# Language-model tower on one core: identity products on TensorE moved in the first expert attention and added in the latent stage

## What is computed

```python
h = tok_embedding_with_layernorm(ids)            # 4096 tokens, 192 features
h = h + L0_attn(layernorm(h))                    # fake-quantised attention, 12 heads
h = h + L0_ffn(layernorm(h))                     # gate stage: 3 "experts" of causal attention, top-2 gate
h = h + L1_attn(layernorm(h))                    # latent stage
h = h + L1_ffn(layernorm(h))                     # routed stage: attention, then 8 experts, top 2

# L1_attn (latent stage)
latent = silu(rmsnorm(x) @ w_comp)               # 192 -> 128
q, k, v = split(latent @ w_qkv); gates from latent @ w_reso
out = decayed linear attention(q, k, v, gate)    # 12 heads of 16
x = x + rmsnorm(out) @ w_proj * silu(latent @ w_outgate)
x = x + (silu(xn @ w1) * (xn @ w2)) @ w3         # xn = rmsnorm(x), hidden 512

# L1_ffn (routed stage)
x = x + softmax(q k^T / 4) v @ out_proj          # 12 heads of 16, 128 tokens a sequence
xm = layernorm(x); top 2 of softmax(xm @ router) choose experts
x = x + sum of gelu(xm @ w1[e] + b1[e]) @ w2[e] + b2[e], weighted
```

## Time and profile before

| | |
|---|---|
| Three runs | 1986.03, 1988.45, 1989.02 us; median 1988.45 |
| Profiled execution: its own time | 1987.9 us |
| its span, first to last instruction | 1986.2 us, 36888 instructions |
| TensorE busy, share of the span | 1551.4 us, 78% |
| VectorE busy | 1311.0 us, 66% |
| ScalarE busy | 959.7 us, 48% |
| GpSimd busy | 400.6 us, 20% |
| Mean granted TensorE clock | 0.881 of full |

### The profile page before, as it was taken

One profiled execution on the slowest core, in us unless ns is written; L12 is line 12 of the kernel. 1 busy time (PEld: TensorE's weight loads), 2 busy tenths in 40 slices (PEclk: granted clock), 3 DMA queues, 4 the chain that ended last, 5 costly groups with the idle time before them and its releaser, 6 DMA issues.

```text
span 1986.2 us, 36888 instructions
## 1 busy us (share of the span) xinstructions
PE 1551.4 (78%) x12764; PEld 1187.1 (60%) x12764; DVE 1311.0 (66%) x4361; ACT 959.7 (48%) x2769; POOL 400.6 (20%) x494
## 2 busy tenths in 40 slices
PE   0076764888888667887888868999999949999996
PEld 0032221776666445565555546777777738888885
DVE  7898885787888768878888844666666632222221
ACT  1275999863444544454454423444434324444442
POOL 7401332000000100000000000222222223333332
PEclk9985555569999779989999988999999959999998
DMA  3000000119990000000000000000000027778875
GB/s 75 17 1 1 1 1 1 22 42 185 180 164 5 1 0 1 0 0 0 0 0 0 0 24 3 26 25 24 24 24 24 25 88 181 193 199 192 194 192 141
DMA packets 136264, 113.02 MB, mean 57 GB/s; under 512 B 29417, under 2 KB 128457, under 8 KB 136137
## 3 DMA queue, kind: packets, MB, share of 16 engines
q1 hardware_dynamic: 119320, 91.70, 20.2%
q0 software_dynamic: 16864, 20.33, 5.3%
HBM read 69.19 MB, written 45.94 MB: 58 GB/s over the span
## 4 chain that ended last, share of the span: by engine, by line
PE 44%; DVE 37%; ACT 12%; issue 4%; POOL 1%; DVEq 0%; DMA 0%; ACTq 0%; POOLq 0%; SPq 0%
ACT bank L716 9%; PE bank L2357 8%; PE bank L2347 6%; PE bank L1007 5%; PE bank L2342 3%; PE bank L1000 3%; PE bank L2012 3%; DVE R L1588 2%; DVE WK L1588 2%; DVE R L1864 2%; PE bank L2025 1%; PE bank L2040 1%; PE bank L1712 1%; PE bank L966 1%; PE bank L640 1%
## 5 line engine op out<-in xcount | busy, mean ns | idle before, releaser
L1047 POOL TENSOR_TENSOR WK<-WK,mhalf 128x2 f32<-128x2 f32 (+1 forms) x96 | 78.0, 812 | 806.9 <-DVE WK L1512 324.5
L2394 ACT ACTIVATE R<-bank,R 128x256 f32<-128x256 f32 x234 | 98.2, 471 | 187.3 <-PE bank L2347 185.5
L716 ACT ACTIVATE bank<-bank,nbias,sc 128x128 f32<-128x128 f32 x384 | 168.9, 993 | 21.3 <-POOL nbias L528 21.3
L2274 POOL DMA_INDIRECT moe_sum<-WK x78 | 121.5, 1557 | 229.0 <-DMA moe_sum<-WK 165.3
L2245 DVE SCALAR_TENSOR_TENSOR WK<-bank,R,WK 128x192 f32<-128x192 f32 x78 | 28.9, 413 | 209.4 <-PE bank L2357 209.4
L716 ACT ACTIVATION_READ_ACCUMULATOR bank<-bank,nbias,sc 128x1 f32 x384 | 163.2, 768 | 0.0
L2357 PE MATMUL bank<-R 128*128 128x192 f32 x936 | 158.6, 326 | 0.0
L1007 PE MATMUL bank<-WK,R 96*128 96x256 f32 x576 | 148.3, 400 | 6.5 <-ACT WK L973 3.8
L2357 PEld LDWEIGHTS bank<-R 128*128 128x128 f32 x936 | 151.3, 190 | 0.0
L1007 PEld LDWEIGHTS bank<-WK,R 96*128 96x128 f32 x576 | 106.9, 195 | 26.2 <-ACT WK L973 6.9
L2347 PE MATMUL bank<-R 128*128 128x256 f32 x468 | 112.8, 392 | 0.0
(11 more groups left out here) (499 smaller groups left out, 3996.9 us busy)
## 6 DMA issues: line engine op xcount, KB each, us to landing
moe_rows_in<-zeros SPq DMA_DIRECT2D x1, 25026.0 KB, 148.2
R<-in_L_ffn_w SPq DMA_DIRECT2D x39, 576.0 KB, 5.0
R<-in_L_ffn_w SPq DMA_DIRECT2D x39, 384.0 KB, 3.1
R<-moe_rows_in SPq DMA_DIRECT2D x39, 194.0 KB, 4.6
R<-in_L_ffn_w SPq DMA_DIRECT2D x78, 96.0 KB, 3.6
R<-in_L_ffn_b SPq DMA_DIRECT2D x39, 96.0 KB, 5.1
moe_sum<-resid POOLq DMA_DIRECT2D x16, 192.0 KB
moe_sum<-WK POOLq DMA_INDIRECT x78, 5.8
```

The costliest lines, as they stand in the source:

```text
L716: ins = nc.scalar.activation(s, s, ACT.Exp, bias=nbias[:, u, k:k + 1], scale=col(SS), accum_out=units(sum_all, g, u)[:, k:k + 1])
L2274: pool.indirect_dma_start(out=acc, out_offset=bass.IndirectOffsetOnAxis(ap=x_id[k % B3][:, t:t + 1].bitcast(U32), axis=0), in_=x_y[k % B3] ...
L2394: ins = nc.scalar.activation(x_hid[q], hidden_at(p, n), ACT.Gelu, bias=xb_1[h][:, q:q + 1])
```

## The change

Two identity products of the latent stage follow the latent product and precede the wait for the Silu; five stand before the wait for `ffn_in`, ahead of the doubled turn. In the routed stage the two at the start of a half turn and the two behind the second block of turned scores go; five (into the other stream's bank 1) stand before the wait for the four exponentials of the first block. That makes 7 a half turn in the latent stage and 16 instead of 15 in the routed stage.

```diff
--- before.py
+++ after.py
@@ -1696,6 +1696,7 @@
             yield
             pe.wait_ge(f.xT, per(g, 3, 1))
             product(a, lw_comp, slice(0, LAT), a.bank[1][:, 0:NM]).then_inc(f.lat_p, 1)
+            stirred_f(a, 2)
             pe.wait_ge(f.lat, per(g, 1, 1))
             for i in range(M):
                 nc.tensor.matmul(a.bank[(2, 0)[i]][:, 0:384], a.lat[:, i * P:(i + 1) * P], lw_cat[:, 0:384], start=True,
@@ -1727,6 +1728,7 @@
             pe.wait_ge(f.xT, per(g, 3, 2))
             token_product(a, lw_proj, 1, f.proj_p)
             yield
+            stirred_f(a, 5)
             pe.wait_ge(f.ffn_in, per(g, 1, 1))
             turn_doubled(a, a.xr, 2, f.xT_p)
             pe.wait_ge(f.xT, per(g, 3, 3))
@@ -2040,7 +2042,6 @@
                 nc.tensor.matmul(a.bank[1][:, 0:P], ident[:, :], ident[:, :], start=True, stop=True)
 
         def tensor_m_1(pe, g, a, f, prev):
-            stirred(a, 2)
             pe.wait_ge(f.x, per(g, 1, 1))
             turn(a, a.xr, 0, f.xT_p)
             yield
@@ -2072,9 +2073,9 @@
             pe.wait_ge(f.topped, per(g, M, M))
             scores(pe, g, a, f, 0, f.scoresT, True)
             yield
+            stirred(streams[1 - a.n], 5)
             pe.wait_ge(f.exp, per(g, 4 * M, 4))
             scores(pe, g, a, f, 1, f.scoresT, True)
-            stirred(streams[1 - a.n], 2)
             pe.wait_ge(f.exp, per(g, 4 * M, 5))
             m_times_v(a, f, 0)
 
```

## The result

The changed kernel takes 1977.88 us (median of 5 runs, 1975.23 to 1979.6), the kernel before 1988.64 on the same chip: ratio 0.9944, 95% interval 0.9932 to 0.9956. So it is 10.8 us faster. It is close to rival D, at 1977.1, but not for rival D's reasons, as the last part shows.

What follows compares the result with a forecast made beforehand. No engine alone bounds the kernel, work passing between TensorE and VectorE; the change can win only through TensorE's clock. 1987.9 - 3.4 (routed clock) - 1.6 (latent clock) + 0.8 (direct cost) = 1983.7 us, range 1979.5 to 1989.5.

Steps and rivals of the forecast that it cites:

- rival D: Both stages: all clock falls vanish, 1987.9 - 7.4 - 4.2 + 0.8 = 1977.1 us; chance 0.10.
- The routed cover: Routed stage, five products before the exponentials' wait: second score block 0.25 to 0.35 us late, turn not later, cost 0.
- The latent cover: Latent stage, five products ahead of the doubled turn: 0.75 us delay inside 0.87 us of wait; 0.8 us booked in all.
- what the clock gives back in the routed stage: Routed stage: present falls recovered, -7.4 us; new falls in two or three of eight half turns, +4.0; net -3.4.
- The latent gain: Latent stage: clock falls behind the doubled turn and a shorter second one go, -1.6 us; ends 0 and -4.2.
- B: Both stages: clock falls as often as before, gains about nil, direct costs remain, 1988.7 us; chance 0.25.
- C: Routed stage: emptied stretch ahead of the turn brings a fall in every longer-wait half turn, 1993.3 us; chance 0.10.

Runs made afterwards that it cites:

- the four kept: Against the kernel before, routed stage only: five products added before the wait for the exponentials, the four others left in; 1981.1 us, ratio 0.995.
- the kernel with ten: Against the changed kernel: ten products instead of five ahead of the latent stage's doubled turn; its one run took 1989.1 us.
- three in the wait: Against the changed kernel: three products instead of five before the wait for the exponentials; 1978.4 us, ratio 0.9949 to the kernel before.
- the four taken away: Against the kernel before: the routed stage's four products removed, none put before the wait for the exponentials; 2000.2 us, ratio 1.0052.
- the routed-only kernel: Against the kernel before: only the routed stage changed, four products removed and five put before the wait for the exponentials; 1981.6 us, ratio 0.9953.

## Why the prediction was wrong

**What held.** The change can win only through the clock: the lengths at full clock are the same in both stages to 0.02 us. The routed cover: the second block is late (0.45 us, I had 0.25 to 0.35), and the turn behind it is not. That it would cost 0.3 us where no wait takes it up was shown with the four kept: 0.27. The latent cover: 0.74 us of delay inside 0.87; with ten products the rest came out, 0.85 and 0.68 a half turn. (The sum as I wrote it, 918.54 + 8 x 0.215, is 920.26 and not 920.37; the 0.87 is borne out by the 1.83 us of the kernel with ten.) The 0.8 us booked there were 0.

**The step that failed: what the clock gives back in the routed stage.** I had -7.4 + 4.0 = -3.4; it gave -10.9. Two terms are off.

1. "I expect it in two or three of the eight such half turns", +4.0. None came. The mechanism exists, as three in the wait show (one fall, 1.45 us) and the four taken away too, but with five dense products before it the stretch between second block and turn brought it in none of seven profiles. I took a stretch with much waiting for a sure loss. The trace had an answer to this that I gave no weight: of the eight falls before, seven start 11.7 to 13.2 us after their mark, at the second block and what follows it directly, and the eighth, in the first half turn, in the wait ahead of that block. Rival D had this and got 0.10.
2. "Eight of 24.60 and seven of 23.84 would be 363.7", so 7.4 for the clock. The first half turn has less work (21.92), the third (24.26) and the last (24.21) take a little less than 24.60 at full clock, and the true sum is 360.2. 3.5 us of the clock's cost were hidden in half turns that looked of normal length. A floor has to be taken from half turns with the same work; for the first one the record count of its row showed it (224 against 252), which is 2.7 of the 3.5; the other two have the full count. The two terms, 4.0 and 3.5, are the 7.5 us between -3.4 and -10.9. Over the whole program the profiled executions differ by 10.0 us where the forecast had 4.2: 7.5 more in the routed stage and the 0.8 booked for nothing, less 1.0 in the latent stage and 1.5 in stretches that I had as unchanged.

**The latent gain** was put at -1.6: the falls behind the doubled turn do vanish, and the difference of the means over profiles is -1.8, but the profiled execution has -0.6, because the falls at the loop's end hit it twice. Whether the latent part of the change is worth nothing, about 2 us or the 4.4 of its own run is not settled: the changed kernel has ratios of 0.9944 and 0.9953 and the routed-only kernel 0.9953, which cannot be told apart.

**Rivals.** B (no gain) is out. C's fall is real but rare. D was right for the routed stage, and wrong for the latent one, where only one kind of fall vanished. That its 1977.1 comes so near to the measured 1977.9 is luck: it took -7.4 for the routed clock, which was -10.9, and -4.2 for the latent one, which was -0.6 in the profile, and the errors cancel. Putting the range's low end at 1979.5 left D out although both its ends were bounds that no row excluded.

Not tried: which of the two routed removals matters, and the four at L1599 without the other seven.

## What to carry to other kernels

Find where each fall of TensorE's clock starts, counted from a mark of the loop, and put the products into the wait that lies just before that place, as many as the wait holds: here 16 a half turn gave 360 us with five at the right place and 397 with these at the wrong one, and 11, with none at either, 378. Then look for the next place; here it was worth another 6 to 7 us by the runs, 4.8 in the profiles. Take the floor of a stage from half turns with the same work (a lower record count is one sign that it is not the same), and give back products where no wait follows them.

## What was not expected of the hardware

- Ten transposes in the wait for the exponentials hold the clock where five products did, in 360.3 against 360.3 us, and nothing there gave 378.0.
- Products behind the poor stretch are worse than none, 396.9 against 378.0 us: they run at half clock themselves (2.3 us for five) and lie on TensorE's path.
- The latent stage took 439.3 to 443.3 us in the profiles of six kernels that do not change it, by how many falls came. The same kind of half turn has a fall in one pass and none in the next; the routed stage without a fall repeats to 0.2 us in seven profiles (360.2 to 360.3).
